# Output products of an attention over two packed groups of heads instead of four

## The chip, the cores and the metric

The kernel runs on one core of a Trainium2 chip. The metric is the device time of one execution in microseconds (us). Three timed runs of the kernel before gave 2165.13, 2165.31 and 2165.94 us.

## The reference

A two-layer decoder works on one sequence of T = 2048 rows of D = 256 values. Each layer has a mixing block, a cross attention and a feed-forward block, each added to the rows and followed by a layer norm. Both cross attentions have 16 heads of 16 values; the context has 1601 rows, and in layer 0 only the context rows with a nonzero mask count:

```python
scores = einsum('bhsd,bhed->bhse', q, k) * DH ** -0.5     # 16 heads, DH = 16
attn = softmax(where(mask == 0, -inf, scores), axis=-1)   # layer 0; no mask in layer 1
out = einsum('bhse,bhed->bhsd', attn, v)
x = layernorm(x + out.reshape(b, s, H * DH) @ Wo.T)       # layer 1 adds a bias b_out
```

The output product (`@ Wo.T`) contracts over 16 x 16 = 256 values.

## The kernel before

Rows are held feature-major: X is 128 partitions x 2 halves x 2048 tokens, worked in NC = 4 chunks of CH = 512 tokens. `attend` (L816) is built for both attentions. Layer 0 takes at run time a window of 4 key tiles of 128 (a branch on the mask; this input fits it), layer 1 all 13 tiles. Below they are called the windowed and the wide attention.

The 16 heads are worked in G = 4 groups of HG = 4. A *unit* is one group of one chunk, so there are 16 units in an attention. Scores come out keys x tokens. For each key tile of a unit TensorE makes four score products (L1195) into a ring of three PSUM banks (5 to 7), ScalarE takes their exponentials (L1276), and four value products (L1173) add into bank 4, one head in each 32 partitions. A head's V tile, a column block of `Vaug`, is 32 wide: 16 columns of values, a column of ones (L988) whose product is the softmax denominator, and 15 columns of zeros. So a unit's sum has for each head 16 rows of values, one of the denominator and 15 of zeros.

Beside this TensorE makes score products in the other orientation for units ahead ("items", L1130), in two alternating slots of two banks (0 to 3); VectorE reduces them to maxima (L1324 windowed, L1327 wide), cuts the turned maxima into three bf16 parts (L1340 to L1346), and SyncE stores those into the rows of the next scores' operand. A slot is free again once VectorE has read it (`slot_free`).

When a unit's values are summed, during the next unit: ScalarE copies bank 4 to `Osb` (L1255; two buffers, by turns of the units); TensorE spreads the four denominators over their 32 rows with one product (`denominators`, L1181); ScalarE takes the logarithm (L1259) and, after one more exponential, exp(-x) of it (`invert`, L1263); GpSimd multiplies `Osb` by that into `On[:, group]` (`normalise_o`, L1307). After the fourth group of a chunk TensorE makes the output product (`out`, L1225), once for each half m of the 256 outputs:

```python
for g in range(G):
    ins = eng.matmul(slot_banks(s_static)[:, 0, :], wo_w[:, g, m * P:(m + 1) * P],
                     On[:, g, :], start=g == 0, stop=g == G - 1)
```

Rows of `wo_w` that stand against a denominator or zeros are zero (the weights are loaded 16 rows in every 32, L324 and L1514, over a cleared tile). VectorE adds the result to X (L1364) and frees the slot.

The order on each engine is written out by `plan(u)` (L1001). Unit 0 stands alone, units 1 to 4 of a pass are the body of a loop that runs three times (`run_units`, L1072), units 5 to 7 follow. `out` stands in unit 4 behind key tile `AT_OUT`: behind the last tile of the windowed unit, behind tile 11 of 13 of the wide one. So three of a chunk's output products lie in the loop, and the fourth is made at the end of an attention, when TensorE has nothing else left. Each engine's queue is in order; semaphores are counted, and TensorE waits for `o_norm` ahead of `out`.

Before unit 0 there is a prologue: SyncE loads keys and rows of ones, stores Q's three bf16 parts as they are cut and loads them back (`load_q`, L1091); the first items run; TensorE makes V tiles (L1147) from item `VALUES_FROM` on and ScalarE copies each into `Vaug` (L1291), before which GpSimd has cleared `Vaug` (L983) and set the column of ones.

Of the kernel before, what the change touches and what calls it, by code (L numbers as in the profile page):

```python
# [12 lines left out]
ALU = mybir.AluOpType  # L13
# [36 lines left out]
ARENA = 53208  # L50
ROWS = 100
# [66 lines left out]
def decoder(nc, io):  # L118
    with ExitStack() as ctx:
# [88 lines left out]
        Vaug = f32(a0, NKT, H, 32)  # L208
        a0 += NKT * H * 32
        parts = bf16(a0, 2, 3, 2, CH)  # L210
        On, Osb = f32(a0, HG, CH), f32(a0 + G * CH, 2, CH)
# [19 lines left out]
        a0 += 2 * CH  # L231
        assert a0 <= ARENA, a0

# [72 lines left out]
        def _(eng):  # L306
# [406 lines left out]
        @part("pe")  # L713
        def _(eng):
            def loaded(eng):
                eng.wait_ge(ld_early[0], 16)
                eng.wait_ge(ld_xw[0], 16 * (1 + HG))

            early_keys[0].products(eng, xatt[0]["WK"], loaded)
# [96 lines left out]
        def attend(a, ready, wq, wv, wo_w, ld_w, bias, banks_free, all_free, keys_free, ctx_free,  # L816
# [50 lines left out]
            v_mm, v_in = count("v_product", NKT), count("v_placed", NKT)  # L867
            v_clear, v_keep = count("v_cleared", 1), count("v_keep_column", 1)
# [3 lines left out]
            const_rows = count("constant_rows", 16 * 4)  # L872
# [9 lines left out]
            den_inv, o_norm = count("den_inverse", units), count("o_normalised", units)  # L882
# [3 lines left out]
            def _(eng):  # L886
# [26 lines left out]
                all_free(eng)  # L913
                for i in range(4):
# [40 lines left out]
            def _(eng):  # L955
                banks_free(eng)
                eng.wait_ge(ld_w, 16 * (1 + HG))
# [23 lines left out]
            def _(eng):  # L981
# [89 lines left out]

            def run_units(eng, unit):  # L1072
# [50 lines left out]
            def _(eng):  # L1123
# [15 lines left out]
                def value_tile(t):  # L1139
# [4 lines left out]
                    if t >= 4:  # L1144
                        v_in.wait(eng, t - 3)
# [5 lines left out]
                const_rows.wait(eng, 16 * 4)  # L1151
# [16 lines left out]
                v_keep.wait(eng, 1)  # L1168
                v_in.wait(eng, n_kt)
# [8 lines left out]
                def denominators(u, i, r):  # L1178
                    ring_wait(eng, u, i, r)
                    o_copied.wait(eng, i)  # L1180
                    eng.matmul(ring_bank(r), pick_den, Osb[:, (u - 1) % 2, :], start=True,  # L1181
                               stop=True).then_inc(ring_full.sem, 1)

                def unit(u, c):
# [4 lines left out]
                    for step in plan(u):  # L1189
# [35 lines left out]
                def out(m, s_static, s_count, units):  # L1225
                    if m == 0:
                        o_norm.wait(eng, units)
# [12 lines left out]
                for m in range(2):  # L1240
                    out(m, s + m, s + m + 2 * SLOTS, 16)
# [8 lines left out]
            def _(eng):  # L1250
                def copy_o(u, i):
# [9 lines left out]
                def invert(u, i, r):  # L1261
                    ring_read.wait(eng, ring_before(i) + (r + 1))
                    eng.activation(Rden[:, (u - 1) % 2, :], Rden[:, (u - 1) % 2, :], ACT.Exp, bias=0.0,  # L1263
                                   scale=-1.0).then_inc(den_inv.sem, 1)

                def unit(u, c):
                    i = unit_of(u, c)
                    to_invert = None
                    for step in plan(u):
# [14 lines left out]
                        elif step == ("pv", n_kt - 1, -1):  # L1284
                            copy_o(u, i)
                    assert to_invert is None

                v_keep.wait(eng, 1)
# [6 lines left out]
                copy_o(16, 16)  # L1295
                log_den(16, 16, 0)
                invert(16, 16, 0)

            @part("pool")
            def _(eng):  # L1300
                def normalise_o(u, c, i):
# [5 lines left out]
                    eng.tensor_tensor(On[:, (u - 1) % 4, :], Osb[:, (u - 1) % 2, :], Rden[:, (u - 1) % 2, :],  # L1307
# [898 lines left out]
```

## Time and profile before

| | |
|---|---|
| timed runs, median (lowest to highest) | 2165.31 us (2165.13 to 2165.94) |
| profiled execution, its own time | 2165.84 us |
| its span, first to last instruction | 2164.0 us |
| mean granted TensorE clock | 0.938 |
| TensorE busy (matmuls) | 1849.4 us, 85% of the span |
| VectorE, ScalarE, GpSimd busy | 1080.7, 932.6, 305.5 us |
| windowed attention, scores to last update of X | 341.6 to 576.7 us |
| wide attention, the same | 1024.4 to 1676.1 us |

The table is from the profile's head and from answers of its trace. Busy time of TensorE is modelled at its ends, so neighbouring matmuls overlap in the record; distances between starts are the safer measure. One float32 matmul instruction leaves two records in the trace.

### The profile page before, as it was taken

What the parts mean: (1) busy time and instruction counts of PE and PEld (TensorE: products, weight loads), DVE (VectorE), ACT (ScalarE), POOL (GpSimd) and SP (SyncE); (2) the same over time, 40 slices, a digit from 0 to 9 for tenths busy, and PEclk for the clock granted to TensorE, in tenths of its full rate; (3) what the DMA queues carried; (4) which work ended last, traced back from release to release, by engine and by line L of the source; (5) the groups of instructions that cost most, each with busy time, mean ns of one, the idle gap of its engine ahead of it and who ended that gap; (6) DMA issues with size and microseconds to landing.
All of it is one profiled execution on the core that took longest, in us unless ns stands there. A gap on an engine that the chain in (4) does not pass through costs nothing.

```text
span 2164.0 us, 27413 instructions
## 1 busy us (share of the span) xinstructions
PE 1849.4 (85%) x7552; PEld 796.6 (37%) x7553; DVE 1080.7 (50%) x1554; ACT 932.6 (43%) x1663; POOL 305.5 (14%) x236
## 2 busy tenths in 40 slices
PE   6889968999799785768999999999998529999994
PEld 2334423333244232324333333333332416666663
DVE  4663348777121233448887687688770402222223
ACT  3331236767510324423777577577676101221221
POOL 4134011000300200331000000000000241111111
PEclk9989989999999887889999999999999659999997
DMA  6001023110100200417000000000000921111113
GB/s 234 24 32 47 0 67 78 30 30 16 55 0 0 85 19 0 50 31 138 9 9 16 9 9 16 9 9 16 1 1 0 381 79 28 28 28 27 27 29 90
DMA packets 65839, 95.09 MB, mean 44 GB/s; under 512 B 11078, under 2 KB 59526, under 8 KB 63824
## 3 DMA queue, kind: packets, MB, share of 16 engines
q1 hardware_dynamic: 58736, 84.66, 13.4%
q0 software_dynamic: 7008, 9.25, 2.6%
q8 instruction: 50, 0.82, 0.2%
q14 instruction: 45, 0.37, 0.1%
HBM read 63.18 MB, written 30.30 MB: 43 GB/s over the span
## 4 chain that ended last, share of the span: by engine, by line
PE 56%; DVE 6%; issue 5%; ACT 2%; POOL 2%; DMA 1%; DVEq 0%; ACTq 0%; POOLq 0%; SPq 0%
PE ps L516 10%; PE ps L1830 9%; PE ps L1173 8%; PE ps L1195 8%; PE ps L1130 8%; PE ps L1845 5%; DVE arena L1327 2%; PE ps L1477 2%; PE ps L440 1%; POOL rows_in L1942 1%; PE ps L1230 1%; PE ps L1838 1%; ACT arena L1898 1%; PE ps L1824 1%; PE ps L1799 1%
## 5 line engine op out<-in xcount | busy, mean ns | idle before, releaser
L1276 ACT ACTIVATE arena<-ps 128x512 f32<-128x512 f32 x1088 | 575.2, 600 | 224.6 <-PE ps L1195 223.1
L1327 DVE TENSOR_REDUCE arena<-ps 128x1 f32<-128x802 f32 (+1 forms) x512 | 480.5, 986 | 121.1 <-PE ps L1130 120.3
L516 PE MATMUL ps<-arena 128*128 (+1 forms) x832 | 387.9, 625 | 73.4 <-DVE arena L1629 23.2
L1195 PE MATMUL ps<-arena 100*128 100x512 bf16 x1088 | 369.8, 384 | 14.0 <-issue 5.8
L1130 PE MATMUL ps<-arena 97*128 97x401 bf16 (+2 forms) x1280 | 339.6, 348 | 27.9 <-issue 19.3
L1173 PE MATMUL ps<-arena 128*32 128x512 f32 x2176 | 290.9, 607 | 1.4 <-ACT arena L1276 1.4
L516 PEld LDWEIGHTS ps<-arena 128*128 128x128 f32 x832 | 165.2, 201 | 288.3 <-issue 286.0
L1830 PE MATMUL ps<-arena 128*128 x608 | 197.9, 468 | 29.1 <-ACT arena L1898 29.1
L1195 PEld LDWEIGHTS ps<-arena 100*128 100x128 bf16 x1088 | 104.6, 98 | 265.8 <-ACT arena L1276 186.9
L1130 PEld LDWEIGHTS ps<-arena 97*128 97x128 bf16 x1280 | 115.2, 98 | 210.8 <-DVE arena L1327 88.1
L2040 DVE TENSOR_TENSOR arena<-ps,arena 128x352 f32<-128x352 f32 x76 | 39.9, 525 | 268.6 <-ACT arena L1905 197.6
L1324 DVE TENSOR_REDUCE arena<-ps 128x2 f32<-128x1024 f32 x128 | 152.2, 1219 | 36.5 <-PE ps L1130 35.5
L1307 POOL TENSOR_TENSOR arena<-arena 128x512 f32<-128x512 f32 x32 | 40.7, 1270 | 863.1 <-ACT arena L1263 693.9
L1830 PEld LDWEIGHTS ps<-arena 128*128 128x128 f32 x608 | 110.0, 191 | 88.1 <-issue 39.7
L1905 ACT ACTIVATE arena<-ps 128x352 f32<-128x352 f32 x76 | 35.3, 464 | 181.9 <-PE ps L1830 181.9
L1845 PE MATMUL ps<-arena 128*128 x456 | 112.4, 387 | 0.8 <-ACT arena L1911 0.8
L1951 POOL DMA_INDIRECT sums<-arena x38 | 59.2, 1559 | 315.0 <-DVE arena L2053 315.0
L486 ACT ACTIVATE arena<-arena x36 | 37.8, 1058 | 136.3 <-DVE arena L453 114.5
L1845 PEld LDWEIGHTS ps<-arena 128*128 128x128 f32 x456 | 83.0, 188 | 30.0 <-issue 13.7
L420 POOL TENSOR_TENSOR arena<-arena x28 | 36.5, 1313 | 364.6 <-DVE arena L1501 132.9
L1898 ACT ACTIVATE arena<-ps 128x256 f32<-128x256 f32 x38 | 14.6, 384 | 156.8 <-PE ps L1824 156.8
L1173 PEld LDWEIGHTS ps<-arena 128*32 128x32 f32 x2176 | 42.8, 108 | 100.5 <-ACT arena L1276 81.4
(196 smaller groups left out, 1465.1 us busy)
## 6 DMA issues: line engine op xcount, KB each, us to landing
arena<-in_experts_w SPq DMA_DIRECT2D x8, 2176.0 KB, 17.7
arena<-qparts SPq DMA_DIRECT2D x192, 64.0 KB, 2.3
qparts<-arena SPq DMA_DIRECT2D x48, 128.0 KB, 2.2
rows_in<-arena SPq DMA_DIRECT2D x1, 5200.0 KB, 17.7
arena<-in_ctxT SPq DMA_DIRECT2D x3, 1664.0 KB, 8.6
kparts<-arena SPq DMA_DIRECT2D x24, 208.0 KB, 2.3
arena<-kparts SPq DMA_DIRECT2D x12, 416.0 KB
arena<-rows_in SPq DMA_DIRECT2D x38, 130.0 KB, 2.1
```

Of the source, the lines that this page charges most:

```text
L516: ins = eng.matmul(out, w[:, k, m * P:(m + 1) * P], x[:, k, tok(c)], start=k == 0, stop=k == ktiles - 1)
L1130: ins = eng.matmul(slot_banks(s_static)[:, x, 0:n_keys], Qst[0:97, ring, heads[x], q * P:(q + 1) * P], Kst[0:97, at_head(ring * HG + heads ...
L1173: ins = eng.matmul(o_bank[32 * h:32 * h + 32, :], Vaug[:, kt, (w % 4) * HG + h, :], probs[:, keys_of(w, kt) % 2, h, :], start=kt == 0, sto ...
L1195: eng.matmul(ring_bank(r), Kst[0:ROWS, at_head(g * HG + h), kt * P:(kt + 1) * P], Qst[0:ROWS, g, h, :], start=True, stop=True).then_inc(ri ...
L1276: eng.activation(probs[:, keys_of(u, kt) % 2, h, :], ring_bank(r), ACT.Exp, bias=0.0).then_inc(ring_read.sem, 1)
L1307: eng.tensor_tensor(On[:, (u - 1) % 4, :], Osb[:, (u - 1) % 2, :], Rden[:, (u - 1) % 2, :], ALU.mult).then_inc(o_norm.sem, 1)
L1324: eng.tensor_reduce(Mneg[:, par, :].rearrange("p (h q) -> p h q", q=QT)[:, heads[0]:heads[0] + 2, q], got, AX.X, ALU.max, negate=True).the ...
L1327: eng.tensor_reduce(MX[:, par, heads[0] * QT + q, n % 2:n % 2 + 1], got, AX.XY, ALU.max).then_inc(slot_free.sem, 1)
L1477: ins = eng.matmul(ps[:, 4 + m, :], ffn["down"][:, j, m * P:(m + 1) * P], ffn_h[:, j, :], start=j == 0, stop=j == FK - 1)
L1830: ins = eng.matmul(ps[:, 2 * half + w, 0:HALF], rowsT[:, u, k, :], experts_all[:, bass.ds(expert * EW + ((2 * w + k) * FE + half * HALF), ...
L1845: ins = eng.matmul(ps[:, 7, 0:D], hiddenT[0:m, i, :], experts_all[0:m, bass.ds(expert * EW + (4 * FE + i * D), D)], start=i == 0, stop=i = ...
L1951: eng.indirect_dma_start(sums[:, :], bass.IndirectOffsetOnAxis(ap=slot_id[:, u:u + 1], axis=0), y[:, u, :], None, compute_op=ALU.add).then ...
```

## The change

Heads of two groups share a 32-row block. In groups 0 and 2 a head's values stay in rows 0 to 15 of its 32 and the denominator in row 16; in groups 1 and 3 the values move to rows 16 to 31 and the denominator to row 0. GpSimd multiplies an even group into `On[:, q]` as before; an odd group it multiplies in place in `Osb`, and then adds to `On[:, q]`. `On` has two entries instead of four, the weights are packed in the same way, and `out` has two matmuls for each half instead of four.

For this the row of the denominator must become zero: exp(-x) gets a bias of -200 in those rows (`den_bias`, one column for each kind of group), which four small VectorE instructions make from `pick_den` and from a second spreading matrix `pick_odd`, loaded by SyncE with two more DMAs in each attention's prologue. The copy of a V tile becomes two (even and odd groups), the setting of the ones four copies instead of one; the weights come by eight DMAs of half the size instead of four. Counts of semaphores follow.

```diff
@@ sync, at the start (and the same at L1514 for the second attention)
             for j in range(HG):
-                eng.dma_start(out_w[0][32 * j:32 * j + DH, :, :],
-                              io["w_out0"][:, j, :, :].rearrange("g i n -> i g n")).then_inc(ld_xw[0], 16)
+                for r in range(2):
+                    eng.dma_start(out_w[0][32 * j + DH * r:32 * j + DH * (r + 1), 0:2, :],
+                                  io["w_out0"].rearrange("(q r) j i n -> q r j i n", r=2)[:, r, j, :, :]
+                                  .rearrange("q i n -> i q n")).then_inc(ld_xw[0], 16)
...
@@ attend, sync
                 all_free(eng)
+                eng.dma_start(pick_odd[0:P - DH, :], io["pick_den"][DH:P, :]).then_inc(const_rows.sem, 16)
+                eng.dma_start(pick_odd[P - DH:P, :], io["pick_den"][0:DH, :]).then_inc(const_rows.sem, 16)
...
@@ attend, pool, prologue
-                eng.tensor_copy(Vaug_w[:, :, :, DH], keep_cols.unsqueeze(2).broadcast_to([P, n_kt, H]))\
-                    .then_inc(v_keep.sem, 1)
+                for r in range(2):
+                    for g in range(r, G, 2):
+                        ins = eng.tensor_copy(Vaug_w[:, :, g * HG:(g + 1) * HG, 0 if r else DH],
+                                              keep_cols.unsqueeze(2).broadcast_to([P, n_kt, HG]))
+                    ins.then_inc(v_keep.sem, 1)
...
@@ attend, pe
-                    eng.matmul(ring_bank(r), pick_den, Osb[:, (u - 1) % 2, :], start=True,
+                    eng.matmul(ring_bank(r), (pick_den, pick_odd)[(u - 1) % 2], Osb[:, (u - 1) % 2, :], start=True,
                                stop=True).then_inc(ring_full.sem, 1)
...
-                            out(step[1], s, s + shift(u, c), i)
+                            out(step[1], s, s + shift(u, c), normalised(u, c))
...
-                    for g in range(G):
-                        ins = eng.matmul(slot_banks(s_static)[:, 0, :], wo_w[:, g, m * P:(m + 1) * P],
-                                         On[:, g, :], start=g == 0, stop=g == G - 1)
+                    for q in range(2):
+                        ins = eng.matmul(slot_banks(s_static)[:, 0, :], wo_w[:, q, m * P:(m + 1) * P],
+                                         On[:, q, :], start=q == 0, stop=q == 1)
...
@@ attend, act
                     if u >= 3:
-                        o_norm.wait(eng, i - 2)
+                        o_norm.wait(eng, normalised(u, c, 2))
...
-                    eng.activation(Rden[:, (u - 1) % 2, :], Rden[:, (u - 1) % 2, :], ACT.Exp, bias=0.0,
-                                   scale=-1.0).then_inc(den_inv.sem, 1)
+                    eng.activation(Rden[:, (u - 1) % 2, :], Rden[:, (u - 1) % 2, :], ACT.Exp,
+                                   bias=den_bias[:, (u - 1) % 2:(u - 1) % 2 + 1], scale=-1.0).then_inc(den_inv.sem, 1)
...
-                    eng.activation(Vaug[:, t, :, 0:DH], ps[:, 4 + t % 4, 0:D].rearrange("p (h d) -> p h d", h=H),
-                                   ACT.Copy, scale=keep_cols[:, t:t + 1]).then_inc(v_in.sem, 1)
+                    for r in range(2):
+                        eng.activation(Vaug_pairs[:, 2 * t:2 * t + 2, r, :, DH * r:DH * (r + 1)],
+                                       ps[:, 4 + t % 4, 0:D].rearrange("p (q r j d) -> p q r j d", r=2, j=HG, d=DH)
+                                       [:, :, r, :, :], ACT.Copy, scale=keep_cols[:, t:t + 1]).then_inc(v_in.sem, 1)
...
@@ attend, pool, normalise_o
-                    eng.tensor_tensor(On[:, (u - 1) % 4, :], Osb[:, (u - 1) % 2, :], Rden[:, (u - 1) % 2, :],
-                                      ALU.mult).then_inc(o_norm.sem, 1)
+                    g, rden = (u - 1) % 4, Rden[:, (u - 1) % 2, :]
+                    if g % 2 == 0:
+                        eng.tensor_tensor(On[:, g // 2, :], Osb[:, 0, :], rden, ALU.mult).then_inc(o_norm.sem, 1)
+                    else:
+                        eng.tensor_tensor(Osb[:, 1, :], Osb[:, 1, :], rden, ALU.mult).then_inc(o_norm.sem, 1)
+                        o_norm.wait(eng, normalised(u, c) - 1)
+                        eng.tensor_tensor(On[:, g // 2, :], On[:, g // 2, :], Osb[:, 1, :], ALU.add).then_inc(o_norm.sem, 1)
...
@@ attend, dve
+                const_rows.wait(eng, 16 * 6)
+                for r, pick in enumerate((pick_den, pick_odd)):
+                    eng.tensor_reduce(den_bias[:, r:r + 1], pick, AX.X, ALU.max).then_inc(den_bias_set.sem, 1)
+                for r in range(2):
+                    den_bias_set.wait(eng, 2)
+                    eng.tensor_scalar(den_bias[:, r:r + 1], den_bias[:, r:r + 1], UNUSED_ROW, None, ALU.mult)\
+                        .then_inc(den_bias_set.sem, 1)
```

## Rows read from the trace of the kernel before

**Rows 1.** The page's chain of work that ended last, by line.
```profile
PE ps L516 10%; PE ps L1830 9%; PE ps L1173 8%; PE ps L1195 8%; PE ps L1130 8%; PE ps L1845 5%; DVE arena L1327 2%; PE ps L1477 2%; PE ps L440 1%; POOL rows_in L1942 1%; PE ps L1230 1%; PE ps L1838 1%; ACT arena L1898 1%; PE ps L1824 1%; PE ps L1799 1%
```
**Rows 2.** Stretches: length, busy PE, PEld, DVE, ACT, POOL, granted clock, DMA share, GB/s.
```profile
345.50:567.20 221.70, 213.85 (x1083) 66.54 (x1081) 152.31 (x179) 159.65 (x300) 20.31 (x16) 1.00 0.12 36
1064.00:1180.00 116.00, 115.50 (x670) 38.17 (x669) 93.65 (x111) 85.33 (x165) 3.81 (x3) 1.00 0.04 12
```
**Rows 3.** The same of L1230 alone: length, PE, PEld, granted clock, DMA share, GB/s.
```profile
404.38:411.37 6.99, 6.99 (x16) 2.95 (x16) 1.00 0.21 56
567.08:575.76 8.68, 8.68 (x16) 3.54 (x16) 0.80 0.00 1
1668.15:1675.14 6.99, 6.99 (x16) 2.95 (x16) 1.00 0.00 0
```
**Rows 4.** Order of time, windowed units: start, length, engine, line, [idle before <-releaser].
```profile
382.18 0.60 ACT L1255 ACTIVATE arena<-ps 128x512 f32<-128x512 f32 x1 [0.33 <-PE ps L1173]
...
394.77 0.60 ACT L1255 ACTIVATE arena<-ps 128x512 f32<-128x512 f32 x1 [0.33 <-PE ps L1173]
...
398.33 1.27 POOL L1307 TENSOR_TENSOR arena<-arena 128x512 f32<-128x512 f32 x1 [11.32 <-ACT arena L1263]
...
404.38 7.15 PE L1230 MATMUL ps<-arena 128*128 128x512 f32 x16
...
408.24 0.69 DVE L1364 SCALAR_TENSOR_TENSOR arena<-ps,arena 128x512 f32 x1 [3.48 <-PE ps L1230]
...
411.87 2.15 ACT L1276 ACTIVATE arena<-ps 128x512 f32<-128x512 f32 x4 [7.67 <-PE ps L1195]
...
414.34 0.60 ACT L1255 ACTIVATE arena<-ps 128x512 f32<-128x512 f32 x1 [0.32 <-PE ps L1173]
```
**Rows 5.** Order of time on ScalarE: the copy of a unit's sum, three wide units.
```profile
1141.34 0.60 ACT L1255 ACTIVATE arena<-ps 128x512 f32<-128x512 f32 x1 [0.29 <-PE ps L1173]
...
1180.01 0.60 ACT L1255 ACTIVATE arena<-ps 128x512 f32<-128x512 f32 x1 [0.29 <-PE ps L1173]
...
1230.30 0.60 ACT L1255 ACTIVATE arena<-ps 128x512 f32<-128x512 f32 x1 [0.70 <-PE ps L1173]
```
**Rows 6.** The chain in order of time at the wide loop's return: start, length, what.
```profile
1223.26 2.64 issue
```
**Rows 7.** Stretches as in rows 2, where the granted clock was low.
```profile
567.30:570.70 3.40, 3.40 (x5) 1.34 (x5) 0.00 (x0) 1.28 (x1) 0.00 (x0) 0.50 0.01 2
1226.10:1229.45 3.35, 3.35 (x12) 1.11 (x14) 1.87 (x2) 2.13 (x4) 0.00 (x0) 0.50 0.16 45
```
**Rows 8.** Order of time, end of the wide attention.
```profile
1666.13 0.63 ACT L1263 ACTIVATE arena<-arena 128x512 f32<-128x512 f32 x1
...
1666.84 1.26 POOL L1307 TENSOR_TENSOR arena<-arena 128x512 f32<-128x512 f32 x1 [27.55 <-ACT arena L1263]
...
1668.15 7.15 PE L1230 MATMUL ps<-arena 128*128 128x512 f32 x16 [2.69 <-POOL arena L1307]
...
1675.34 0.75 DVE L1364 SCALAR_TENSOR_TENSOR arena<-ps,arena 128x512 f32<-128x512 f32 x1 [2.69 <-PE ps L1230]
...
1676.39 1.26 POOL L420 TENSOR_TENSOR arena<-arena  x1 [8.29 <-DVE arena L1364]
```
**Rows 9.** Groups by line and shape: busy, mean ns of one, idle before.
```profile
L1291 ACT ACTIVATE arena<-ps,arena 128x256 f32<-128x256 f32 x17 | 8.1, 476 | 27.6 <-PE ps L1147 27.6
...
L1898 ACT ACTIVATE arena<-ps 128x256 f32<-128x256 f32 x38 | 14.6, 384 | 156.8 <-PE ps L1824 156.8
...
L1592 ACT ACTIVATE arena<-ps,arena 128x512 f32 x8 | 5.1, 685 | 44.1 <-PE ps L516 44.1
```
**Rows 10.** Order of time, prologue of the wide attention.
```profile
957.48 1.13 SPq L915 DMA_DIRECT2D arena<-in_ones  x4
...
962.65 1.33 SPq L908 DMA_DIRECT2D qparts<-arena  x3
...
1023.77 0.48 ACT L1291 ACTIVATE arena<-ps,arena 128x256 f32<-128x256 f32 x1 [1.32 <-PE ps L1147]
...
1024.35 0.38 PE L1195 MATMUL ps<-arena 100*128 100x512 bf16 x1 [0.61 <-issue]
```

More of the change, by code:

```diff
@@ L50 @@
 ARENA = 53208
+UNUSED_ROW = -200.0
 ROWS = 100
@@ L207, in decoder @@
         a0 += 2 * HG * CH
-        Vaug = f32(a0, NKT, H, 32)
+        Vaug, Vaug_pairs = f32(a0, NKT, H, 32), f32(a0, NKT * 2, 2, HG, 32)
         a0 += NKT * H * 32
         parts = bf16(a0, 2, 3, 2, CH)
-        On, Osb = f32(a0, HG, CH), f32(a0 + G * CH, 2, CH)
+        On, Osb = f32(a0, 2, CH), f32(a0 + G * CH, 2, CH)
         a0 += (G + 2) * CH
@@ L231, in decoder @@
         a0 += 2 * CH
+        pick_odd, den_bias = f32(a0, P), f32(a0 + P, 2)
+        a0 += P + 2
         assert a0 <= ARENA, a0
@@ L881, in attend @@
             o_copied = count("o_copied", units)
-            den_inv, o_norm = count("den_inverse", units), count("o_normalised", units)
+            den_inv, o_norm = count("den_inverse", units), count("o_normalised", units + units // 2)
+            den_bias_set = count("den_row_bias", 4)
             @part("sync")
@@ L1070, in chunk_of, with normalised @@
                 return (c + u // 4) if 1 <= u <= 4 else (0 if u == 0 else 3)
+            def normalised(u, c, back=0):
+                k = u - back
+                return 6 * c + k + k // 2 if 1 <= u <= 4 else 12 + k + k // 2
             def run_units(eng, unit):
@@ L1144, in value_tile @@
                     if t >= 4:
-                        v_in.wait(eng, t - 3)
+                        v_in.wait(eng, 2 * (t - 3))
                     for k in range(2):
@@ L1167, in _ @@
                         s += 1
-                v_keep.wait(eng, 1)
-                v_in.wait(eng, n_kt)
+                v_keep.wait(eng, 2)
+                v_in.wait(eng, 2 * n_kt)
                 def values(w, kt):
@@ L1221, in unit, with out @@
                         elif what == "out":
-                            out(step[1], s, s + shift(u, c), i)
+                            out(step[1], s, s + shift(u, c), normalised(u, c))
                             s += 1
-                def out(m, s_static, s_count, units):
+                def out(m, s_static, s_count, normalised):
                     if m == 0:
-                        o_norm.wait(eng, units)
+                        o_norm.wait(eng, normalised)
                     slot_free.wait(eng, s_count - 1)
-                    for g in range(G):
-                        ins = eng.matmul(slot_banks(s_static)[:, 0, :], wo_w[:, g, m * P:(m + 1) * P],
-                                         On[:, g, :], start=g == 0, stop=g == G - 1)
+                    for q in range(2):
+                        ins = eng.matmul(slot_banks(s_static)[:, 0, :], wo_w[:, q, m * P:(m + 1) * P],
+                                         On[:, q, :], start=q == 0, stop=q == 1)
                     ins.then_inc(slot_full.sem, 1)
@@ L1240, in _ @@
                 for m in range(2):
-                    out(m, s + m, s + m + 2 * SLOTS, 16)
+                    out(m, s + m, s + m + 2 * SLOTS, normalised(8, 0))
             def chunk_of_next(u, c, ahead):
@@ L1262, in invert @@
                     ring_read.wait(eng, ring_before(i) + (r + 1))
-                    eng.activation(Rden[:, (u - 1) % 2, :], Rden[:, (u - 1) % 2, :], ACT.Exp, bias=0.0,
-                                   scale=-1.0).then_inc(den_inv.sem, 1)
+                    eng.activation(Rden[:, (u - 1) % 2, :], Rden[:, (u - 1) % 2, :], ACT.Exp,
+                                   bias=den_bias[:, (u - 1) % 2:(u - 1) % 2 + 1], scale=-1.0).then_inc(den_inv.sem, 1)
+                den_bias_set.wait(eng, 4)
                 def unit(u, c):
@@ L1314, in _ @@
                 run_units(eng, unit)
-                normalise_o(16, 0, 16)
+                normalise_o(8, 0, 16)
             @part("dve")
             def _(eng):
+                const_rows.wait(eng, 16 * 6)
+                for r, pick in enumerate((pick_den, pick_odd)):
[4 more added lines that the diff above has]
+                        .then_inc(den_bias_set.sem, 1)
                 def item(par, n, s_static, s_count):
@@ L1513, in _ @@
             for j in range(HG):
-                eng.dma_start(out_w[1][32 * j:32 * j + DH, :, :],
-                              io["w_out1"][:, j, :, :].rearrange("g i n -> i g n")).then_inc(ld_xw[1], 16)
+                for r in range(2):
+                    eng.dma_start(out_w[1][32 * j + DH * r:32 * j + DH * (r + 1), 0:2, :],
+                                  io["w_out1"].rearrange("(q r) j i n -> q r j i n", r=2)[:, r, j, :, :]
+                                  .rearrange("q i n -> i q n")).then_inc(ld_xw[1], 16)
             eng.wait_ge(spare_set, 2)
```

25 lines of the change are left out of this document (12 added, 13 removed).

## The prediction

> **What bounds the kernel now.** I read the chain of waits first. It runs mostly through TensorE, and the output product's line L1230 has a rounded 1% of it [rows 1], somewhere between 11 and 32 us; that is too coarse for a sum, and the chain charges part of a stall to the engine that waited. So I went to the stretches. In both attentions TensorE is busy nearly throughout: 213.85 of 221.70 us in the windowed one and 115.50 of 116.00 us in three wide units that hold no output product, at a granted clock of 1.00, while VectorE stays at 152 and 94 us and ScalarE at 160 and 85 us [rows 2]. There, time that leaves TensorE's queue should leave the span, unless a wait takes its place.
>
> The order of time tests that. In the windowed loop the copy of a unit's sum (L1255) starts at 382.18, 394.77 and 414.34: a unit takes 12.59 us, and the one that holds `out` 19.57, so 6.98 us more [rows 4]. L1230 alone takes 6.99 us for its 16 records [rows 3]. All of it is paid; nothing hides there. Meanwhile VectorE sat idle for 3.48 us ahead of its first update of X and ScalarE 7.67 us ahead of its next exponential [rows 4]: both wait for the product. The wide units take 38.67 us, and the one with `out` 50.29 [rows 5]. Of those 11.62 us extra some 7 are `out`; the rest is the loop's return, where TensorE waits 2.64 us for nothing that the profile shows [rows 6] and then has half its clock for 3.4 us [rows 7]. That stays.
>
> **The change part by part.**
>
> *Half the output products.* A chunk's `out` is 8 matmuls in 16 records, 6.99/16 = 0.437 us each [rows 3]. It becomes 4 matmuls in 8 records, over the same 128 rows and 512 columns as before, since the zero rows were multiplied too: 8 x 0.437 = 3.49 us less for each chunk. Six of the eight stand inside loops (three in each attention): 6 x 3.49 = 20.9 us. What is late next there? The first half's slot is needed again by the next item. That half is now through 3.49 us after 404.38, at 407.87, and VectorE's update runs from 408.24, 0.37 later, for 0.69 us [rows 4]. With half the records it is through after 1.75 us and its update ends 0.37 + 0.69 later, at 2.81; the next item comes at 3.49 at the earliest. Some 0.7 us remain, so no new wait; if that cover failed, the price is at most the update itself, 0.75 us [rows 8], for each half.
>
> *One more GpSimd instruction for an odd group.* The add is a 128x512 float32 operation on the engine and line of the multiply, 1.27 us [rows 4]. Inside the loops it is covered: GpSimd's multiply for the fourth group ends at 399.60 and `out` begins at 404.38 [rows 4], a lead of 4.78 us, of which the add takes 1.27 + 0.08 (the hand-over from ScalarE's 1666.76 to GpSimd's 1666.84 [rows 8]); 3.4 us stay. The wide lead is longer, since `out` stands nine key tiles after the denominators. Without the cover it would cost 1.35 us for each `out`. `Osb`'s buffer is held until the add at most, while its next copy comes two units later (25 us).
>
> At the two ends it is on the path: TensorE waits 2.69 us for GpSimd [rows 8]. There the add costs 1.35 us and `out` gives back 3.49.
>
> *A bias column in exp(-x).* The trace has no such L1263. Nearest: an activation with a bias column of the same size, 685 ns [rows 9], against 0.60 us for L1255 [rows 4]: 0.09 us more. Bounds: nothing, and 0.09 for all 32 units, 2.9 us. In the loops ScalarE waits for TensorE in each unit, so I charge it at the two ends only, 0.09 each.
>
> *V tiles in two copies.* A copy of 256 columns into `Vaug` takes 476 ns, 384 without the scaling column and the stride [rows 9]. From 384 ns for 256 columns and 0.60 us for 512, a column costs 0.84 ns; half a tile is then about 0.37 us, a pair 0.74, 0.26 more than now. At worst a half costs as much as a whole, 0.48 more. Between V copies ScalarE idles 1.32 us [rows 10], so all tiles but the last are covered. The last is not: its copy ends at 1024.25 and the first score of unit 0 starts at 1024.35 [rows 10]. I take 0.3 us for each attention, 0.5 at worst; 0.6 us in all. If no tile were covered: 17 x 0.48 = 8.2 us.
>
> *The small things in the prologue.* SyncE issues two more DMAs ahead of the rows of ones: four such take 1.13 us from 957.48, and the next issue comes at 962.65 [rows 10], so there are 4 us of room for about 0.6. Without it the store of Q's parts would start that much later, at most 0.9 in each attention. VectorE's four small instructions and their wait fall before Q is back from DRAM, ahead of any item. The four copies of ones run on GpSimd, which then waits for Q's parts; V tiles come some 7 or 19 items later. The eight weight loads instead of four carry the same bytes, two stages before their use; behind them in SyncE's queue stand the mask row (needed only after the first norm) and the clearing of rows that waits for the feed-forward block. I charge nothing for these; together they cannot exceed 2 x 0.9 + about 1 us.
>
> *The sum*, against the profiled execution's own 2165.84 us (span 2164.0 and 1.84 around it): loops -20.9; ends 2 x (-3.49 + 1.35 + 0.09) = -4.1; V copies +0.6: -24.4, so 2141.4. The median of the runs shown is 0.5 lower, 2165.31, so I say 2140.9.
>
> *The clock at the ends.* The end of the windowed attention had half the clock for 567.30 to 570.70 [rows 7], and its `out` took 8.68 instead of 6.99 us [rows 3]; the wide one's kept 1.00 after 2.69 us of waiting [rows 8]. Now both waits grow to 4.0 us. If the windowed half-rate stretch stays where it is, `out` begins 1.4 us further into it and meets less of it, some 0.7 us better than the sum (half of 1.4). If both new products ran at half rate altogether, each for 2 x 3.49 = 6.98 us, the wide end would lose 6.98 - 6.99 + 1.44 = 1.4 us and the windowed one give 8.68 - 6.98 - 1.44 = 0.3: 1.1 us lost instead of 4.1 won, 5.2 us worse. The Trainium skill ("TensorE: Matmul & The Clock Gate", *What's actually happening*) says that the throttled state is the default and only activity releases it, which speaks against a change that lengthens a wait; the trace agrees at the windowed end and not at the wide one. By that rule the time would be that of the first rival.
>
> **The rivals.**
>
> 1. *The longer wait costs the clock at both ends.* As just worked out, 2140.9 + 5.2 = 2146.1. For it: the windowed end, and the half clock behind the 2.64 us at the wide loop's return [rows 6, 7]. Against: the wide end kept its clock after the same 2.69 us.
>
> 2. *VectorE takes TensorE's place.* If the next item waits for the update of X, each of the 12 halves in the loops costs 0.75 us: 9 us back, 2149.9. For it: the margin of 0.7 us is small. Against: VectorE has nothing else queued then, it idled 3.48 us just before [rows 4].
>
> 3. *The products take as long as the rows they fill.* A product over 128 filled rows might cost twice one over 128 rows half zero; then the loops gain nothing, and the ends pay 1.44 each: 2165.3 + 2.9 + 0.6 = 2168.8, no change that can be told. Against: the instruction always streamed 128 rows by 512 columns, and the record of a product says nothing of what the rows hold; but no row here sets a filled product of this shape beside it.
>
> 4. *Slower: the throttle takes the loops.* With fewer dense products in each chunk the granted clock falls inside the loops. A half-rate stretch of 3.4 us cost 1.69 us (8.68 against 6.99 [rows 3]); between 14 and 15 more such stretches eat the 24.4 us, from where on the change loses; with four in each of the eight chunks the time is 2140.9 + 32 x 1.69 = 2195. Against: three wide units without any output product ran at 1.00 throughout [rows 2].
>
> **How the numbers follow.** Forecast 0.77, rival 1 0.10, rival 2 0.07, rivals 3 and 4 0.03 each. The forecast's own range is 2137.5 to 2145: below by the 0.7 us at the windowed end and up to 2 x 1.69 us if the wide loop's returns keep their clock; above by the 2.9 us of bias columns and 0.9 in a prologue. Rival 1 and most of rival 2 end below 2149, so 2137.5 to 2149 holds about 0.86. About 0.2% (4.3 us) is what a measurement of this kernel can tell from no change. Faster by more than that: forecast and rivals 1 and 2, 0.94. Within: 0.03. Slower: 0.03.
>
> **What would show it.** In the changed kernel's trace: 64 records of the output product at an unchanged 0.43 to 0.44 us from start to start; windowed units with `out` at about 16.1 us beside 12.6 without, wide ones 3.5 us shorter than 50.3; no idle time of TensorE ahead of `out` in the loops that GpSimd ends; GpSimd's two instructions at the ends 1.35 us apart and TensorE's wait there 4.0 to 4.1 us; L1263's successor at about 0.72 us; V copies twice as many with TensorE's first score 0.3 us later behind them. I am wrong if units without `out` grow, if the unit with `out` shrinks by much less than 3.5 us, or if a half-rate stretch appears in the loops outside their returns.

## The result and the profile after

The changed kernel takes 2151.6 us (median of 4 runs, 2149.88 to 2152.79) beside 2165.62 us of the kernel before (4 runs, 2165.13 to 2170.66): 0.9929 of it, 95% interval 0.9912 to 0.9947. That is 14.0 us less, where 24.4 were forecast, and it lies above the range given. Run again later, beside the experiments, it gave 0.9917 (0.9898 to 0.9935).

The profiled execution took 2149.88 us (span 2148.0, mean granted clock 0.936); it is the fastest of the four, so it shows 16.0 us less and not 14.0. Cut at ScalarE's copies of the units' sums and at the ends of VectorE's updates of X, the two spans compare as follows; the last column is a run told below, with both missed costs taken away.

| stretch | before, us | forecast | after | repaired (e7) |
|---|---|---|---|---|
| start to the windowed attention's first copy | 357.00 | +0.3 | -1.49 | -1.04 |
| first to last copy, windowed | 205.55 | -10.5 | -3.69 | -9.71 |
| last copy to last update of X, windowed end | 14.10 | -2.05 | -1.06 | -3.70 |
| to the wide attention's first copy | 487.30 | +0.3 | +1.08 | -0.93 |
| first to last copy, wide | 599.67 | -10.5 | -10.42 | -10.70 |
| last copy to last update of X, wide end | 12.47 | -2.05 | -0.32 | -2.00 |
| to the end of the span | 487.90 | 0 | -0.07 | +1.12 |
| sum | 2164.0 | -24.4 | -16.0 | -27.0 |

The wide loop gave what was forecast, and five more runs with the same wide loop took 588.89 to 589.18 us for it; in a second profile of the changed kernel it took 592.05, with 6.8 us of half clock behind each return of the loop in place of 3.4. The windowed loop gave a third of its share (201.84 us in the second profile), and each end less than its share. Here are the copies in the windowed loop, then in the wide one (start, length, engine, line, idle before; L1271 is L1255 of before):

```profile
355.51 0.60 ACT L1271 ACTIVATE arena<-ps 128x512 f32<-128x512 f32 x1 [0.32 <-PE ps L1189]
368.10 0.60 ACT L1271 ACTIVATE arena<-ps 128x512 f32<-128x512 f32 x1 [0.32 <-PE ps L1189]
381.65 0.60 ACT L1271 ACTIVATE arena<-ps 128x512 f32<-128x512 f32 x1 [0.41 <-PE ps L1189]
394.32 0.60 ACT L1271 ACTIVATE arena<-ps 128x512 f32<-128x512 f32 x1 [0.40 <-PE ps L1189]
411.34 0.60 ACT L1271 ACTIVATE arena<-ps 128x512 f32<-128x512 f32 x1 [0.32 <-PE ps L1189]
...
1136.18 0.60 ACT L1271 ACTIVATE arena<-ps 128x512 f32<-128x512 f32 x1 [0.30 <-PE ps L1189]
1174.85 0.60 ACT L1271 ACTIVATE arena<-ps 128x512 f32<-128x512 f32 x1 [0.30 <-PE ps L1189]
1221.35 0.60 ACT L1271 ACTIVATE arena<-ps 128x512 f32<-128x512 f32 x1 [0.81 <-PE ps L1189]
```

Windowed units now take 12.59, 13.55, 12.67 and, with `out`, 17.02 us from start to start, where all without `out` took 12.59 and the one with it 19.57 [rows 4]. Every second unit is longer by about 0.9 us: those in which GpSimd has two instructions. The wide units are as before, 38.67, and 46.50 with `out` against 50.29 [rows 5]. So the thing to look for is what GpSimd's second instruction meets in the windowed attention and not in the wide one. First GpSimd, then VectorE, in the long unit that ends at 381.65 (L1331 is the multiply of an odd group, L1333 the add; L1373 to L1379 are the four steps that cut the maxima into three bfloat16 parts, L1357 the reductions of the items):

```profile
371.75 1.27 POOL L1331 TENSOR_TENSOR arena<-arena 128x512 f32<-128x512 f32 x1 [11.23 <-ACT arena L1279]
373.10 1.28 POOL L1333 TENSOR_TENSOR arena<-arena 128x512 f32<-128x512 f32 x1
...
372.24 0.28 DVE L1373 CAST arena<-ps 16x128 bf16<-16x128 f32 x1 [0.37 <-PE ps L1153]
372.55 0.28 DVE L1375 TENSOR_TENSOR arena<-ps,arena 16x128 f32<-16x128 f32 x1
372.86 0.23 DVE L1377 CAST arena<-arena 16x128 bf16<-16x128 f32 x1
373.13 1.38 DVE L1379 TENSOR_TENSOR arena<-arena 16x128 bf16<-16x128 f32 x1
374.44 2.34 DVE L1357 TENSOR_REDUCE arena<-ps 128x2 f32<-128x1024 f32 x2
```

VectorE's last step reads two tiles in SBUF (`arena<-arena`). It starts 0.03 us after the add and ends 0.14 us after it: 1.38 us for 16 x 128 elements. In the kernel before no record of this step (L1346) took over 281 ns, and that kernel's trace shows why: in the same unit the multiply ran from 373.15 for 1.27 us, to 374.42, and the step began at 374.60.

```profile
373.15 1.27 POOL L1307 TENSOR_TENSOR arena<-arena 128x512 f32<-128x512 f32 x1 [11.23 <-ACT arena L1263]
...
374.60 0.28 DVE L1346 TENSOR_TENSOR arena<-arena 16x128 bf16<-16x128 f32 x1
```

The next reductions come about a microsecond late, the slots of the items come free late, and TensorE waits for them. In a table of TensorE's waits over this loop (line, releaser, sum in us, times, longest) two rows are new; before, no wait there ended with VectorE or a DMA. The DMA is the store of the cut maxima in the last unit: it was issued at 542.04, right behind a held step that ended at 541.97.

```profile
PE ps L1146 <- DVE arena L1357: 2.7, 6, 0.5
PE ps L1211 <- DMA arena<-arena: 1.2, 1, 1.2
```

Over the loop TensorE is busy for 193.54 of 201.86 us. Before it was 201.50 of 205.55. Its idle time doubled, at a granted clock of 1.00 in both (before, then after; columns as in [rows 2]):

```profile
357.00:562.55 205.55, 201.50 (x1016) 62.79 (x1014) 142.12 (x167) 149.44 (x282) 19.04 (x15) 1.00 0.12 36
355.51:557.37 201.86, 193.54 (x992) 57.74 (x990) 149.88 (x167) 151.33 (x281) 27.96 (x22) 1.00 0.12 37
```

The ends answer to [rows 8]; here the wide one, GpSimd, TensorE and VectorE's second update of X, and under it stretches of the half clock at the windowed and the wide end (length, PE, PEld, DVE, ACT, POOL, granted clock, DMA share, GB/s):

```profile
1651.35 1.26 POOL L1331 TENSOR_TENSOR arena<-arena 128x512 f32<-128x512 f32 x1 [27.59 <-ACT arena L1279]
1652.69 1.26 POOL L1333 TENSOR_TENSOR arena<-arena 128x512 f32<-128x512 f32 x1
...
1654.01 5.40 PE L1246 MATMUL ps<-arena 128*128 128x512 f32 x8 [4.12 <-POOL arena L1333]
...
1659.44 0.75 DVE L1397 SCALAR_TENSOR_TENSOR arena<-ps,arena 128x512 f32<-128x512 f32 x1 [0.97 <-PE ps L1246]
```
```profile
561.87:568.70 6.83, 5.36 (x7) 2.25 (x8) 0.69 (x1) 1.28 (x1) 1.33 (x2) 0.50 0.01 1
1654.10:1657.60 3.50, 3.50 (x5) 1.44 (x6) 0.00 (x0) 0.00 (x0) 0.00 (x0) 0.51 0.00 0
```

TensorE waited 4.12 us, as forecast, and then had a granted clock of 0.50 (1.2 GHz) for 3.5 us of `out` at the wide end, which had kept its clock before; at the windowed end the half clock came during the wait already and held for 6.83 us. The eight records of `out` took 5.40 us at the wide end and 6.34 us at the windowed one, in place of the 3.71 us that they took in a loop.

### The profile page after: what moved, and what is told of

Read it like the earlier page. It is cut to its first block, busy times and chain, and to the rows that moved or that the text cites. A ratio compares the mean times of both kernels' runs of the same rounds, so it can differ in the third digit from the quotient of the medians.

```text
span 2148.0 us, 27362 instructions
## 1 busy us (share of the span) xinstructions
PE 1828.6 (85%) x7488; PEld 786.0 (37%) x7489; DVE 1089.3 (51%) x1562; ACT 937.7 (44%) x1680; POOL 326.2 (15%) x258
## 4 chain that ended last, share of the span: by engine, by line
PE 57%; DVE 6%; issue 4%; ACT 3%; POOL 2%; DMA 1%; DVEq 0%; ACTq 0%; POOLq 0%; SPq 0%
PE ps L521 10%; PE ps L1189 9%; PE ps L1865 9%; PE ps L1211 9%; PE ps L1146 8%; PE ps L1880 5%; DVE arena L1360 2%; PE ps L1510 2%; PE ps L445 1%; POOL rows_in L1977 1%; PE ps L1873 1%; PE ps L1246 1%; ACT arena L1933 1%; PE ps L1859 1%; PE ps L1197 1%
## 5 line engine op out<-in xcount | busy, mean ns | idle before, releaser
L1357 DVE TENSOR_REDUCE arena<-ps 128x2 f32<-128x1024 f32 x128 | 151.4, 1217 | 34.4 <-PE ps L1146 33.8
L1329 POOL TENSOR_TENSOR arena<-arena 128x512 f32<-128x512 f32 x16 | 20.3, 1270 | 452.2 <-ACT arena L1279 252.6
L1933 ACT ACTIVATE arena<-ps 128x256 f32<-128x256 f32 x38 | 14.6, 383 | 156.7 <-PE ps L1859 156.7
```

The lines of the kernel that those rows point to most:

```text
L1357: eng.tensor_reduce(Mneg[:, par, :].rearrange("p (h q) -> p h q", q=QT)[:, heads[0]:heads[0] + 2, q], got, AX.X, ALU.max, negate=True).the ...
```

## The experiments

Theory A for the windowed loop: GpSimd's add and a VectorE step with two inputs in SBUF exclude each other, and the step waits for the rest of the add. Theory D for the ends: half clock after the longer wait. The first four runs go beside one set of runs of the kernel before (2169.06 us, 9 runs), the last four beside another (2168.7 us, 11 runs). Both are some 3 us above the 2165.62 of the first comparison, and the changed kernel itself ran again only beside the last four. So the first four are read by their ratios and, more finely, by the stretches of their profiles.

**e1: the add later.** In the windowed attention the add waits until the maxima are cut.

```diff
                         o_norm.wait(eng, normalised(u, c) - 1)
+                        if window and u < 7:
+                            max_part.wait(eng, 3 * (i + 2))
                         eng.tensor_tensor(On[:, g // 2, :], On[:, g // 2, :], Osb[:, 1, :], ALU.add).then_inc(o_norm.sem, 1)
```

> The changed kernel with GpSimd's add held back, in the windowed attention, until VectorE has cut the maxima of the unit (four steps); nothing else differs. Theory A (the add holds something that VectorE's last step of the cut, with two inputs in SBUF, needs, so that this step takes 1.38 us in place of 0.28): the step is back at 0.28 us, windowed odd units are back at 12.59 us from 13.55 and, with the chunk's turn, at about 16.1 us from 17.0; seven such units give 6.6 us, so 2151.6 falls to about 2145. Rival B (the odd units are longer for the add's own data, for ScalarE's longer logarithm or for the order of work on TensorE): units stay at 13.5 us and the time within 1.5 us of 2151.6. Rival C (VectorE's step is slow, but the wait is hidden by TensorE's other work): the step falls to 0.28 us and the time stays.

Measured: 2143.99 us (2142.35 to 2145.32), 0.9877 of the kernel before (0.9862 to 0.9893). The same unit, VectorE and GpSimd:

```profile
373.95 0.28 DVE L1381 TENSOR_TENSOR arena<-arena 16x128 bf16<-16x128 f32 x1
374.15 2.34 DVE L1359 TENSOR_REDUCE arena<-ps 128x2 f32<-128x1024 f32 x2
...
374.31 1.27 POOL L1335 TENSOR_TENSOR arena<-arena 128x512 f32<-128x512 f32 x1 [0.47 <-DVE arena L1381]
```

The step is at 0.28 us in all 32 units (282 ns at most); the windowed units are 12.59, 12.68, 12.67 and 16.13 us, and the loop is 6.05 us shorter than after the change (195.81 against 201.86). The same add, some 0.4 us later and beside reductions from PSUM, costs nothing that shows. B and C fall: the add's data and ScalarE's work are the same here.

**e2: a second pass in the kernel before.** Nothing of the change is in it but one more GpSimd instruction behind the first, in every unit.

```diff
                     eng.tensor_tensor(On[:, (u - 1) % 4, :], Osb[:, (u - 1) % 2, :], Rden[:, (u - 1) % 2, :],
+                                      ALU.mult).then_inc(first_pass.sem, 1)
+                    first_pass.wait(eng, i)
+                    eng.tensor_tensor(On[:, (u - 1) % 4, :], Osb[:, (u - 1) % 2, :], Rden[:, (u - 1) % 2, :],
                                       ALU.mult).then_inc(o_norm.sem, 1)
```

> The kernel before, with the normalising multiply on GpSimd made twice in each unit, the second behind a wait for the first; the output products are those of before. Theory A: the second pass takes the place in time of the add, now in all units: in the windowed attention the unit's last step of the cut goes from 0.28 to some 1.3 us and each of the 14 windowed units with a cut is about 0.95 us longer, 13 us in all, and the two ends about 1.3 us longer each: about 2165.6 + 16 = 2181. Wide units stay at 38.66 us. Rival B (the second pass is only a longer way for the normalised rows): the units stay at 12.59 us, only the two ends and the two chunks' turns are longer, 4 x 1.3 at most: 2168 to 2171.

Measured: 2180.44 us (2173.16 to 2184.34), 1.0054 (1.0040 to 1.0068), so 11.4 us more instead of 16. Here GpSimd and VectorE in one windowed unit:

```profile
373.04 1.28 POOL L1311 TENSOR_TENSOR arena<-arena 128x512 f32<-128x512 f32 x1
...
373.14 1.31 DVE L1350 TENSOR_TENSOR arena<-arena 16x128 bf16<-16x128 f32 x1
```

Windowed units now take 13.38 to 13.47 us, even ones too; the loop grew by 11.2 us (216.76), wide units stayed at 38.65, the ends grew by 1.8 and 2.7 us. B falls, and the mechanism is shown without the change: the stretches that the second pass touches grew by 15.7 us, against 16. The total came out smaller in part for the higher kernel before of these runs: 2180.44 is 14.6 above the 2165.84 of its profiled execution. In the profiled execution of e2, the fastest of the five, the wide loop (-3.6 us, its turns at 48.7 and 48.2 us) and the start (-2.3 us) were shorter besides. For the wide loop the clock says why: TensorE idled 2.68 and 2.15 us at its two returns, as it does before (2.64 and 2.58), and then kept a granted clock of 1.00, where before it had half for 3.4 us twice [rows 7]; two such stretches at the 1.69 us of the prediction make 3.4. Here is the stretch behind the first return (columns as there):

```profile
1234.60:1238.00 3.40, 3.40 (x21) 1.29 (x22) 1.93 (x3) 2.74 (x6) 0.00 (x0) 1.00 0.17 52
```

So the half clock behind the returns differs between executions (none here, twice 3.4 us before, twice 6.8 in the second profile of the changed kernel), and moves a total by some 3 us.

**e3: TensorE kept busy at the ends.** 18 score products that nobody reads stand behind the last denominators.

```diff
                 denominators(8, 16, 0)
+                for _ in range(18):
+                    eng.matmul(ring_bank(1), Kst[0:ROWS, 0, 0:P], Qst[0:ROWS, 0, 0, :], start=True, stop=True)
                 s = slots_before(8)
```

> The changed kernel with 18 more score products, whose results nobody reads, on TensorE behind the last denominators of each attention, in the time in which TensorE waits for GpSimd's multiply and add; they add work that is not of the computation. Theory D (the end's output products run at half clock since TensorE stood idle for 4.12 us before them): both ends' products run at full clock, 8 products in 3.6 us in place of 6.34 (windowed) and 5.40 us (wide); about 1.5 us less at the wide end and 2.8 us less at the windowed end, in all 4 us: 2147.6. Rival (the ends are set by the update of X on VectorE and not by TensorE): the records of the products get shorter and the time stays within 1.5 us.

Measured: 2146.63 us (2144.81 to 2148.27), 0.9889 (0.9874 to 0.9904). The wide end's extra products (17 of 18 are in the trace) and its `out`, and the stretch of `out` with its clock:

```profile
1648.59 3.83 PE L1256 MATMUL ps<-arena 100*128 100x512 bf16 x17
1652.66 3.71 PE L1246 MATMUL ps<-arena 128*128 128x512 f32 x8 [0.24 <-POOL arena L1335]
```
```profile
1652.60:1656.40 3.80, 3.71 (x8) 1.44 (x8) 0.75 (x1) 0.00 (x0) 0.01 (x1) 1.00 0.00 0
```

With the clock kept at 1.00 (2.4 GHz), `out` takes 3.71 us, the ends are 2.64 and 1.68 us shorter than after the change (10.40 and 10.47 us), and the update of X follows at once, so its rival falls. But 1.46 us are lost again behind the wide end: the stretch to the end of the span grew from 487.83 to 489.29. It grew by 1.07 to 1.86 in all four runs with shorter ends (e3, e4, e6, e7) and by at most 0.73 in the three others with the ends of the changed kernel (its second profile, e1, e5). At the instruction of ScalarE that stands 12.4 us behind the last update in the changed kernel, the four are 1.14 to 1.29 us late and the three 0.01 us at most. Part of the half clock moved there: the first 5 us behind the last update of X were at 1.00 in the changed kernel and are at 0.78 here:

```profile
1660.19:1665.19 5.00, 3.06 (x6) 0.89 (x6) 1.86 (x3) 0.40 (x1) 4.69 (x4) 1.00 0.62 191
```
```profile
1657.16:1662.16 5.00, 3.16 (x5) 1.26 (x6) 1.22 (x1) 0.41 (x1) 4.70 (x4) 0.78 0.62 180
```

**e4: three products at the end.** The even groups are multiplied with the weights while GpSimd still works; the odd half follows as a product of its own, without the add.

```diff
+                o_norm.wait(eng, normalised(7, 0))
                 for m in range(2):
-                    out(m, s + m, s + m + 2 * SLOTS, normalised(8, 0))
+                    slot_free.wait(eng, s + m + 2 * SLOTS - 1)
+                    for q in range(2):
+                        eng.matmul(slot_banks(s + m)[:, 0, :], wo_w[:, q, m * P:(m + 1) * P], On[:, q, :],
+                                   start=q == 0, stop=False)
+                o_norm.wait(eng, normalised(8, 0))
+                for m in range(2):
+                    eng.matmul(slot_banks(s + m)[:, 0, :], wo_w[:, 1, m * P:(m + 1) * P], Osb[:, 1, :],
+                               start=False, stop=True).then_inc(slot_full.sem, 1)
```

> The changed kernel with another order at each attention's end: the products over the first packed group and over the even half of the second are made while GpSimd still multiplies, and a third product over the odd half (filled rows only for the odd heads) is added in the same bank, so that no add is needed at the end: 6 products of 512 columns for each of 2 slots in place of 4, in halves as before. Theory D and the path of the forecast: the wait is now for the multiply alone (1.35 us less on the path), and only 2 of 6 passes stand behind it at full clock: about 4.6 us less at the wide end and 5.5 us at the windowed end, 2141 to 2142 in all. Rival (the update of X on VectorE, 0.9 us a tile, or the norm's start bounds the ends): less than 3 us in all.

Measured: 2142.3 us (2140.84 to 2143.87), 0.9872 (0.9857 to 0.9887). GpSimd, the two groups of products and VectorE at the wide end:

```profile
1646.67 1.26 POOL L1339 TENSOR_TENSOR arena<-arena 128x512 f32<-128x512 f32 x1 [27.66 <-ACT arena L1287]
...
1645.83 2.74 PE L1260 MATMUL ps<-arena 128*128 128x512 f32 x6
1648.41 1.88 PE L1264 MATMUL ps<-arena 128*128 128x512 f32 x4
...
1649.47 1.61 DVE L1407 SCALAR_TENSOR_TENSOR arena<-ps,arena 128x512 f32<-128x512 f32 x2 [48.85 <-PE ps L1264]
```

The ends shrink to 7.72 and 7.79 us, 5.3 and 4.4 less than after the change. Two of the eight records of the group at 1645.83 are missing from the trace. Again 1.9 us are lost behind the wide end (489.69). The last of this end is now bound by VectorE, whose two updates follow each other without a gap.

**e5: the residual in PSUM.** The add comes when it came, but VectorE's last two steps read the residual from the slot's bank, so that one input is in PSUM.

```diff
+                    left = slot_banks(s_static)[0:16, 1, 0:P]
                     max_part.wait(eng, 3 * i + 1)
-                    eng.tensor_tensor(Mres[0:16, :], src, Mp[0:16, par, 0, :], ALU.subtract).then_inc(slot_free.sem, 1)
+                    eng.tensor_tensor(left, src, Mp[0:16, par, 0, :], ALU.subtract).then_inc(max_part.sem, 1)
...
+                    eng.tensor_tensor(Mp[0:16, par, 2, :], left, Mp[0:16, par, 1, :],
+                                      ALU.subtract).then_inc(slot_free.sem, 1)
```

> The changed kernel with the residual of the cut maxima kept in the slot's bank in PSUM in place of SBUF, so that VectorE's last two steps have one input in PSUM; GpSimd's add comes when it came. The slot is given back two steps later. Theory A1 (what collides is a step of VectorE with two inputs in SBUF while GpSimd works): the last step takes about 0.3 us although GpSimd's add runs beside it, odd windowed units are about 12.6 to 12.7 us, and the time is some 6 us below the changed kernel's of this call. Rival A2 (any step of VectorE that writes SBUF, or any short step beside GpSimd, is held up): the step stays at 1.3 to 1.4 us and the time stays within 1.5 us.

Measured: 2156.3 us (2153.74 to 2160.01), 0.9944 (0.9928 to 0.9960), so 6 us more than the changed kernel beside it (2150.05), not less. Yet the step itself did what A1 says; GpSimd's add and the step, side by side:

```profile
374.53 1.27 POOL L1334 TENSOR_TENSOR arena<-arena 128x512 f32<-128x512 f32 x1
...
374.61 0.28 DVE L1381 TENSOR_TENSOR arena<-ps,arena 16x128 bf16<-16x128 f32 x1
```

0.28 us beside the add, in all units; A2 falls. What the expectation left too small is the slot: it is given back two steps, some 0.6 us, later, and every unit pays for it. In this trace TensorE's items waited 28 times, 7.7 us in all, for the step that now frees the slot; in the changed kernel no matmul waited for the step that frees it there (L1375). Windowed units take 12.99 to 13.08 us (odd ones 0.48 less than after the change, even ones 0.4 more), wide ones 39.15 against 38.66. The windowed loop is 0.83 us shorter than after the change and the wide one 6.04 longer: the remedy cost more than the illness.

**The changed kernel again, e6 (both remedies) and e7 (both missed costs away).** e6 is e1 and e4 together, e7 is e1 and e3.

> The changed kernel itself, unedited, beside the three others, so that their times have a partner of the same chip. Theory A and its rivals expect the same: 0.993 of the kernel before.

> The changed kernel with both edits that helped alone: the add held back in the windowed attention until the maxima are cut (6.0 us from the first to the last copy of the outputs there), and the attention's end in three products without the add (5.4 + 4.4 us, less some 1.4 us that the norm behind gives back at half clock). If they don't share anything, 6.0 + 8.4 = 14.4 us below the changed kernel's time in this call; rival (the half clock that leaves the ends comes back elsewhere in full): 9 us or less.

> The changed kernel with the add held back in the windowed attention and TensorE kept busy at both ends with 18 score products that nobody reads: the two costs that the forecast left out are taken away, and nothing else is altered. If they are all that stands between the forecast and the result, 6.0 + 4.3 - 1.4 = 8.9 us below the changed kernel's time of this call, and about 24 us below the kernel before, the difference that was forecast. Rival (the chunks' turns saved less than forecast, or the start costs more): 4 us or more is still missing, 20 us or less below the kernel before.

Measured: the changed kernel 2150.05 us (2146.75 to 2156.78), 0.9917 (0.9898 to 0.9935). e6: 2134.57 us (2130.81 to 2139.37), 0.9845 (0.9827 to 0.9864), 15.5 us below it against 14.4 expected: the parts add up, and it is the fastest version here. e7: 2142.55 us (2138.86 to 2145.5), 0.9884 (0.9867 to 0.9900), 7.5 us below it against 8.9, and 26.2 below the kernel before (21.7 to 28.8 by the interval), where 24.4 were forecast for the change. Its rival (20 us or less) falls. Beside the same runs the changed kernel is 18.7 us below the kernel before; the 14.0 of the first comparison and these 7.5 would make 21.5, so the total agrees with the forecast to some 3 us and not better. The stretches are surer. With the two costs away they come out as forecast in the table above: -9.71 and -10.70 us for the loops, -2.00 for the wide end. The windowed end gives more, -3.70, since the half clock that it had before is gone too.

## Why the prediction was wrong

The step that failed is the one on GpSimd's second instruction: "Inside the loops it is covered: GpSimd's multiply for the fourth group ends at 399.60 and `out` begins at 404.38 [rows 4], a lead of 4.78 us". The lead is there, and no product waited for the add in a loop. But the sentence asks only who waits for the add's result, not who works beside it. VectorE did, with a step that was held whenever it began inside the add, and seven windowed units paid: 6.05 us by e1, on a term that the sum had at nothing. In the wide attention the maxima are cut at other times than GpSimd works, 14 us or more from it in every unit, so that loop gave its 10.4 us. The first sign of being wrong that the prediction named, units without `out` that grow, is what came.

The Trainium skill has the rule ("SBUF — State Buffer", *SBUF: two separate sides*): GpSimd and VectorE share a pair of ports, and a VectorE instruction with two SBUF inputs or in a two-port mode and a GpSimd instruction hold it by turns, each for the whole instruction, the first to start first. The runs agree: the step ends 0.14 us behind the add, takes 1.38 us in place of 0.28, and 0.28 with one input in PSUM (e5). It speaks against this change and was not weighed. The trace of before had rows that ask for it; two lines of VectorE there, whose maxima stand far off (duration in ns, least, median, most):

```profile
L784 DVE TENSOR_TENSOR arena<-arena x32: 685/694/2485, 156.9 to 262.0; 128x512 f32<-128x512 f32 x32
...
L1344 DVE CAST arena<-arena x32: 214/215/754, 331.7 to 1620.5; 16x128 bf16<-16x128 f32 x32
```

In both the long records ran beside GpSimd: the eleven of L784 that took over 1.1 us (a tile in SBUF multiplied by itself) beside other lines of GpSimd, and the one of L1344 beside the multiply L1307 in the last windowed unit, ending 0.08 us after it.

The second step that failed is the sum at the two ends: "There the add costs 1.35 us and `out` gives back 3.49." The wait came as summed: it grew by 1.43 us (2.69 to 4.12), where 1.35 and 0.09 for the bias column were put down. `out` gave back only 2.50 us at the windowed end (8.84 to 6.34) and 1.75 at the wide one (7.15 to 5.40), since its records at half clock start 0.85 us apart and not 0.43. So the ends gave 1.06 and 0.32 us where 2.05 each were forecast; rival 1, with all of `out` at half clock, had 0.3 won and 1.4 lost. The runs lie between the two. e3, which keeps TensorE busy, took 2.64 and 1.68 us off the ends. As a price for the whole kernel that is too much, since 1.46 us are lost again behind the wide end. The sum took the one end of before that kept its clock after 2.69 us for safe ground. The rule that was cited from the Trainium skill ("TensorE: Matmul & The Clock Gate", *What's actually happening*), that the throttled state is the default and activity releases it, agrees with both ends: the granted clock was 0.50 and 0.51 there after 4.12 us of waiting.

Point by point, the rest: 64 records in place of 128, and the unit with `out` 3.44 us shorter where nothing holds VectorE (16.13 in e1 against 19.57), as forecast. The wait of 4.12 us at the ends against 4.0 to 4.1, the two GpSimd instructions 1.34 us apart against 1.35. The update of X left no new wait: TensorE waits 0.40 us for it in each of the wide loop's three chunks, 1.2 us in all, in both kernels (rival 2 falls, although its time, 2149.9, happens to lie near the result, and lies outside the range that was said to hold most of it); rival 3 falls by the records' length, 0.59 us median in both kernels; rival 4 by a granted clock of 1.00 over the windowed loop. The bias column and the split copies of V, by line and shape (busy us, mean ns, idle before):

```profile
L1279 ACT ACTIVATE arena<-arena 128x512 f32<-128x512 f32 x32 | 23.1, 723 | 0.1
...
L1310 ACT ACTIVATE arena<-ps,arena 128x128 f32<-128x128 f32 x34 | 10.6, 365 | 26.3 <-PE ps L1163 26.3
```

0.72 us is what was said; a pair of copies is 0.73 us, 0.25 more than the one of 476 ns [rows 9]. What it does to the prologues can't be told: the start, up to the first copy, lies between 355.08 and 357.16 us in the eight profiles of kernels that are alike there (355.51 and 356.89 in two profiles of the changed kernel itself). So the +0.3 us for V copies is neither shown nor refuted. The range's lower bound doesn't follow from its own terms either, which give 2140.9 - 0.7 - 3.4 = 2136.8; the result lies at the other side.

Open: in e1 and e7 six of the windowed units still take 12.67 or 12.68 us instead of 12.59, 0.5 us in all. The bias column adds 0.09 us to the same chain, but no run took it out alone. Not known either is why the half clock behind the wide loop's returns lasted 3.4 us in most profiles, 6.8 in one and not at all in e2, after waits of 2.15 to 2.82 us in all of them.

## What to carry to other kernels

An instruction that is covered by the wait for its result can still block its neighbours: before an operation is put on GpSimd, look in the order of time at what VectorE runs in that stretch, and at the inputs of each (two tiles in SBUF, or a cast from SBUF to SBUF). Look also at the longest record of a line and not only its mean: here a lone outlier in the kernel before was a sample of what the change made common. Where a change lengthens TensorE's wait ahead of products at the end of a stage, give it work that is needed anyway to do there, as e4 did. e3's empty work won less, though some 2.7 of the 4.3 us between the two are the add that e4 spares at both ends.

## What was not expected of the hardware

A 16 x 128 step of VectorE (0.28 us alone) was held for 1.1 us by a GpSimd instruction that had started 0.03 us before it, while steps beside it with one input in PSUM took 0.28 us (e5). What was won by keeping the half clock out of the ends was in part lost behind them, where the granted clock of the first 5 us was 0.78 in place of 1.00: 2.64 + 1.68 us won, 1.46 lost (e3). A slot in PSUM given back some 0.6 us later made each unit of both attentions 0.4 to 0.5 us longer (e5), though VectorE is busy for only 142.41 of the windowed loop's 201.03 us there.
